# A graph-and-mixture kernel on one core: the prologue's degree pass shortened, its two roots computed in one chain, and layer 1's last block reordered

## The reference, cut to what matters

```python
xn = _layernorm(x, axis=-1)
x = x + _L0_gnn_ref(xn, edge_index, edge_weight, ...) + _L0_mix_ref(xn[None], ...)[0]
x = x + _L0_ffn_ref(_layernorm(x, axis=-1)[None], ...)[0]

def _gcn_conv(x, edge_index, edge_weight, W, b):      # used twice by _L0_gnn_ref
    ...                                               # self-loops of weight 1 are added
    deg = jax.ops.segment_sum(ew, col, num_segments=n)
    dis = jnp.where(deg > 0, jax.lax.rsqrt(jnp.where(deg > 0, deg, 1.0)), 0.0)
    norm = dis[row] * ew * dis[col]
    h = x @ W.T
    msg = h[row] * norm[:, None]
    return jax.ops.segment_sum(msg, col, num_segments=n) + b

def _block(x, edge_index, edge_weight, g, bln, W, b):
    h = _layer_norm(x, g, bln)
    return x + jax.nn.relu(_gcn_conv(h, edge_index, edge_weight, W, b))
```

## Time and profile before

| | us |
|---|---|
| median of 3 runs (lowest, highest) | 4452.32 (4449.44, 4452.76) |
| the profiled execution's own time | 4450.62 |
| its span, first to last instruction | 4448.9 |
| prologue, up to the first gather | 309 |
| layer 1, up to the first gather of layer 2 | 2038 |
| layer 2 | 2102 |

### The profile page before, as it was taken

How to read it: one execution, slowest core, us unless ns; L and a number is a source line. 1 busy time by engine, 2 the same in 40 slices (tenths; PEclk the granted TensorE clock), 3 DMA queues, 4 the chain that set the end, 5 groups by cost and what they waited for, 6 DMA issues and landing times.

```text
span 4448.9 us, 94972 instructions
## 1 busy us (share of the span) xinstructions
PE 3639.6 (82%) x27016; PEld 3069.7 (69%) x27017; DVE 2477.9 (56%) x8820; ACT 1205.1 (27%) x3172; POOL 3147.3 (71%) x3542
## 2 busy tenths in 40 slices
PE   4876776776776676777777999999999999999998
PEld 3765555655565565555555888888888887888877
DVE  7544544554554554545454665665566665666555
ACT  1330010100100110010013444444444444444434
POOL 4447777777777777777766777777777777777771
PEclk9988888888988888888888999999999999999999
DMA  4034444443444444444443343443344343344431
GB/s 143 29 105 120 130 129 120 129 130 115 129 130 120 128 131 125 125 129 127 119 119 106 116 117 110 118 118 111 114 118 118 110 118 115 114 118 115 117 107 42
DMA packets 256030, 515.37 MB, mean 116 GB/s; under 512 B 61465, under 2 KB 154017, under 8 KB 255969
## 3 DMA queue, kind: packets, MB, share of 16 engines
q0 software_dynamic: 151392, 413.60, 32.8%
q1 hardware_dynamic: 104576, 101.17, 7.0%
HBM read 474.81 MB, written 39.71 MB: 116 GB/s over the span
## 4 chain that ended last, share of the span: by engine, by line
PE 47%; DVE 17%; issue 10%; POOL 8%; DMA 7%; ACT 2%; DVEq 2%; SPq 0%; POOLq 0%; ACTq 0%
PE bank L1199 45%; POOL gs L549 8%; DMA gr<-h_d,idx_r 6%; DVE ss L966 4%; PE bank L1222 1%; DVE rstd L730 1%; DVE rstd L731 1%; DVE rstd L729 1%; DVE st L738 1%; DVEq L966 1%; DVE w L1097 1%; ACT bank L710 1%; DVE u L747 1%; ACT L710 1%; DMA out<-u 1%
## 5 line engine op out<-in xcount | busy, mean ns | idle before, releaser
L549 POOL DMA_INDIRECT gs<-h_d,idx_all x3038 | 2901.9, 955 | 951.3 <-issue 655.6
L1199 PE MATMUL bank<-gs,ss 128*128 128x256 f32 x6272 | 1585.7, 399 | 13.7 <-DMA gs<-h_d,idx_all 12.5
L1199 PEld LDWEIGHTS bank<-gs,ss 128*128 128x128 f32 x6272 | 1210.5, 201 | 191.2 <-DMA gs<-h_d,idx_all 21.5
L966 DVE TENSOR_SCALAR ss<-iw,dst_f,ew 128x128 f32<-128x128 f32 x3152 | 882.4, 358 | 115.8 <-PE bank L1199 67.9
L710 ACT ACTIVATE bank<-bank,eb1c 128x128 f32<-128x128 f32 x1632 | 455.6, 342 | 703.2 <-PE bank L1199 686.3
L1199 PE MATMUL bank<-experts,w 128*128 128x256 f16 x4896 | 616.8, 279 | 23.3 <-DVE w L1097 22.6
L1199 PE MATMUL bank<-w,experts 128*128 128x128 f16 x9792 | 613.8, 219 | 1.2 <-DVE w L1103 1.2
L1199 PEld LDWEIGHTS bank<-w,experts 128*128 128x128 f16 x9792 | 571.1, 98 | 48.7 <-issue 16.6
L1199 PEld LDWEIGHTS bank<-experts,w 128*128 128x128 f16 x4896 | 475.9, 100 | 101.0 <-DVE w L1097 32.6
L1199 PE MATMUL bank<-gr,sr 128*128 128x256 f32 x232 | 114.4, 587 | 449.6 <-DMA gr<-h_d,idx_r 449.4
L1097 DVE SCALAR_TENSOR_TENSOR w<-bank,w 128x512 f16<-128x512 f32 x408 | 280.7, 688 | 279.0 <-ACT w L713 274.5
(11 more groups left out here) (260 smaller groups left out, 3588.2 us busy)
## 6 DMA issues: line engine op xcount, KB each, us to landing
gs<-h_d,idx_all POOLq DMA_INDIRECT x3038
hself<-h_d SPq DMA_DIRECT2D x100, 128.0 KB, 3.3
ew_in<-in_eW SPq DMA_DIRECT2D x49, 168.0 KB, 2.4
out<-u SPq DMA_DIRECT2D x51, 128.0 KB
u<-xn_d SPq DMA_DIRECT2D x50, 128.0 KB
h_d<-u SPq DMA_DIRECT2D x50, 128.0 KB
u<-x_d SPq DMA_DIRECT2D x50, 128.0 KB
u<-r_d SPq DMA_DIRECT2D x50, 128.0 KB
```

What stands on the lines that cost most here:

```text
L549: pool.indirect_dma_start(gs[:, n, :], None, table[:, :], bass.IndirectOffsetOnAxis(ap=idx_all[:, w, n:n + 1], axis=0)).then_inc(s[f"main_ ...
L966: m = dve.tensor_scalar(ss[:, slot + j, :], iw[:, :], dst_f[:, bass.ds(c, 1)], ew[:, bass.ds(c, 1)], ALU.is_equal, ALU.mult)
L1199: return pe.matmul(out_ap, lhsT, rhs, start=first, stop=last, **kw)
```

## The change

It has these parts.

1. **Start of the prologue.** The statistics begin when the first three of the seven transfers of `x` have landed, and are written out instead of looped. Both inverse roots come from one chain of double width (`two`). The scaling of the weights, the copies of `hb`, `w1bias` and `u8` go from DVE to ACT, ahead of `xn_tile(0)`. POOL's addition of 128 to all source indices goes; each gather now has a constant offset (`element_offset`) instead.
2. **The loop over blocks.** POOL no longer copies the indices (DVE does, between L893 and L897) nor the quarter numbers: it subtracts a prepared pair `tile_qn` while it fetches the column. PE's bounds are read after `w6`'s product instead of ahead of it.
3. **End of the prologue.** The last fold stands ahead of block 48's products; DVE, not POOL, takes the last seven inverse roots; the last write of seven blocks is cut into four and three.
4. **Layer 1.** In all blocks the bias of the next row's product is put ahead of its turn (`next_h_bias`). In the last block the last messages and the rest come ahead of `w1`'s products, the next row's products ahead of `w2`'s, the next row is normalised alone, and its store stands ahead of the store of `r`. The waits ahead of `table2` stay.

```diff
             for i in range(0, W, XG):
...
+                             ).then_inc(s["x_first" if i < X_FIRST * XG else "x_in"], 16)
...
-            sp.wait_ge(s["h_dve"], W - H_DVE)
-            h1_rows(W // XG - 1)
+            for t, n in ((H_DVE, 4), (H_DVE + 4, XG - 4)):
+                sp.wait_ge(s["h_dve"], t + n - H_DVE)
+                sp.dma_start(h1_d[(t + 1) * P:(t + n + 1) * P, :].rearrange("(t p) d -> p t d", p=P),
+                             xh[:, t:t + n, :]).then_inc(s["h1_out"], 16)
...
+                if last:
+                    sp.wait_ge(s["h2_done"], W + 1)
+                    sp.dma_start(rows(h2_d, W), u4[:, :]).then_inc(s["h2_out"], 16)
                 sp.wait_ge(s["r_done"], w + 1)
...
-            pc.link(pool.tensor_scalar(src_row[:, :], src_row[:, :], P, None, ALU.add))
...
                 lo = own_column(pool, t)
-                pool.tensor_copy(idx_all[:, bass.ds(t, 1), :].rearrange("p a c -> p (a c)"),
-                                 src_row[:, bass.ds(lo, OWN)]).then_inc(s["idx_listed"], 1)
-                pool.tensor_copy(tile_q, iota_qb[:, bass.ds(t * Q, Q)]).then_inc(s["tile_q_set"], 1)
                 after, off = degree_columns(pool, t)
-                pool.wait_ge(s["tile_q_set"], t + 1)
                 with pool.Fori(after - 1, lo + (OWN - DEG + FRONT), 1) as c:
-                    pool.tensor_copy(own_qn, dst_qn[:, :, bass.ds(c, 1)].rearrange("p a c -> p (a c)")
-                                     ).then_inc(s["rest_own"], 1)
+                    pool.tensor_tensor(own_qn, dst_qn[:, :, bass.ds(c, 1)].rearrange("p a c -> p (a c)"),
+                                       tile_qn[:, bass.ds(t, 1), :].rearrange("p a c -> p (a c)"),
+                                       ALU.subtract).then_inc(s["rest_own"], 1)
...
-            root_seed(2)
-            for _ in range(NEWTON):
-                root_step(2)
-            root_end(2)
...
-                            bass.IndirectOffsetOnAxis(ap=idx_all[:, w, n:n + 1], axis=0)).then_inc(s[f"main_in{n}"], 16)
+                            bass.IndirectOffsetOnAxis(ap=idx_all[:, w, n:n + 1], axis=0),
+                            element_offset=P * D).then_inc(s[f"main_in{n}"], 16)
...
+            act.wait_ge(s["shift_ps"], 3)
+            act.copy(hb[:, 0, :], bank[1][0:1, 0:D])
+            act.copy(hb[:, 1, :], bank[2][0:1, 0:D])
+            act.copy(w1bias[:, :], bank[3][:, 0:HBLK])
+            for k in range(KB):
+                act.activation(w6[:, k, :], w6[:, k, :], ACT.Copy, scale=lncol[:, 0, k:k + 1])
+                act.activation(w7[:, k, :], w7[:, k, :], ACT.Copy, scale=lncol[:, 2, k:k + 1])
+                a = act.activation(w1[:, KB + k, :], w1[:, KB + k, :], ACT.Copy, scale=mixcol[:, 0, k:k + 1])
+            a.then_inc(s["weights_set"], 1)
+            act.wait_ge(s["shift_ps"], 4)
+            act.copy(u8[:, :], wide(2)).then_inc(s["weights_set"], 1)
             act.wait_ge(s["stats_set"], 1)
...
+            both, minus_half, root, tmp = (v[:, :] for v in two)
+            one, onto = slice(0, W), slice(W, 2 * W)
+            ch.link(dve.tensor_scalar(both[:, one], var_all[:, :], EPS, None, ALU.add))
+            ch.link(dve.scalar_tensor_tensor(out=both[:, onto], in0=both[:, one], scalar=EPS, in1=var_all[:, :],
+                                             op0=ALU.mult, op1=ALU.add))
+            inv_sqrt(dve, ch, both, minus_half, root, tmp)
...
+                dve.tensor_copy(idx_all[:, bass.ds(t, 1), :].rearrange("p a c -> p (a c)"),
+                                src_row[:, bass.ds(lo, OWN)]).then_inc(s["idx_listed"], 1)
                 dve.tensor_tensor(oh_node[b], iota_nc.unsqueeze(1).to_broadcast(shape), own_n.unsqueeze(2).to_broadcast(shape),
...
+            inv_sqrt(dve, ch, deg, mh, y, tmp)
+            dve.tensor_tensor(dis[:, 1 + CUTS[2]:], dis[:, 1 + CUTS[2]:], y, ALU.mult).then_inc(s["dis_set"], 1)
             keys(W - 1)
             rows_h(W - 1)
...
+                if last:
+                    z_ins, = layer_norm(dve, tc, (u5[:, :], u3[:, :]))
+                    z_ins.then_inc(s["z1_done"], 1)
+                    dve.wait_ge(s["y1_ps"], w + 1)
+                    y_ins, = layer_norm(dve, tc, (wide(4), t_c[1][:, :]))
...
+                    if last and k == 6:
+                        messages(w, v, PIECES - 1)
+                        rest_messages(*rest_table(pe, 0, w))
...
+                        if last:
+                            next_h_turn(W)
+                            next_h(W)
                         pe.wait_ge(s["hr_done"], HBLK * (w + 1))
```

More of the change, by code:

```diff
@@ L45 @@
 DCOL = NCOL + FRONT
-EDGE_LINKS = 7
+EDGE_LINKS = 6
 HEADS, HD = 8, 32
@@ L62 @@
 XG = 7
+X_FIRST = 3
 CUTS = (0, 4 * XG, 6 * XG, W)
@@ L1068, in window1 @@
                 dve.tensor_tensor(u6[:, :], t_c[1][:, :], t_c[0][:, :], ALU.add).then_inc(s["r_done"], 1)
-                assert tc.n == tc.per, tc.n
+                assert tc.n == tc.per + (LN_LINKS if last else 0), tc.n
             with dve.Fori(0, W - 1) as w:
```

125 lines of the change are left out of this document (65 added, 60 removed).

## The result

| | before | changed |
|---|---|---|
| median of 9 runs (lowest, highest) | 4452.32 (4449.44, 4453.63) | 4439.58 (4436.16, 4440.58) |
| profiled execution's own time, span | 4450.62, 4448.9 | 4436.16, 4434.5 |
| ratio of the times, 95% interval | | 0.9971 (0.9962 to 0.9981) |

A forecast was written before the change was run, and what follows sets the result against it. POOL's gathers were taken to bound layer 1, and a dependent chain the prologue. Terms −9.0 − 10 − 1 + 0 − .5 = −20.5 took 4450.62 to 4430.1, median 4431.8, stated as 4431; range 4420 to 4445.

The forecast's parts named there:

- the first two rivals: Whole kernel: the loop gives only 3, total 4438, chance .20; or the prologue's start gives only 3, 4437, chance .08.
- Start: Start of the prologue, up to PE's first `u,t_b`: 9.0 us gained, bounds 4 and 10.
- The loop: Prologue's loop over blocks: 10 us gained, POOL's part .33 shorter per block, DVE paying .19 for a copy.
- the early mode: Loop's first blocks, POOL ahead: 4.02 becomes 4.2 a block, +2.5 over 13 blocks; then 14 more at 4.2, −7.0.
- the late mode: Loop behind the first roots, POOL late: .1 a block, ten blocks −.9, second roots −1.2, last ones −.3.
- My own sign of being wrong: Any of: early blocks staying at 4.0 or over 4.4, gathers' mean moving over .01, first gather less than 12 earlier.
- the lock: Loop's blocks with POOL late: DVE and POOL exclude each other at a shared port pair, so 2.4 gained instead of 6.
- End of the prologue: From the last block's roots and scalings to the first gather: 1 us gained, bounds 0 and 2.5.
- Layer 1's body: Layer 1's gathers: 0 change, as POOL gets no added instruction; bounds −.02 and +.02 a gather, ∓31.
- Last block: Layer 1's last block: .5 gained, the store of `r` becoming last instead of the new row's; bounds −1.5 and +1.
- The slower rival: Layer 1: the constant offset lengthens each of 1,577 gathers, at .02 each +31.5, total 4462; chance .05.
- POOL stays ahead through the roots: Prologue: the loop gains 17 and the prologue's end 2.5, total 4422; chance .12.

The follow-up runs named there:

- a2: The changed kernel without the gathers' constant offset; POOL adds 128 to the source indices in its preparation as before. Median 4441.54, ratio .9969 of the kernel before.
- a4: The changed kernel with the copy of the source indices in the degree loop moved from DVE back to POOL. Median 4443.39, ratio .9971 of the kernel before.
- a8: The changed kernel with the first two groups' roots moved from POOL to DVE, in four pieces each. 6269.93 against the changed kernel's 6289.92; ratio .9881 of before.
- a1: The changed kernel with the next row's bias product put back behind the turn, ahead of w7's products. Median 4445.05, ratio .9979 of the kernel before.
- a5: The changed kernel with layer 1's last block in its old order, bias still moved; run twice. Medians 6284.76 and 6282.28, ratios .9900 and .9877 of before.

## Why the prediction was right, and where it was not

The direction and the range held, and by its parts the likeliest case; the size was 21 for a measured 12.7. The result, 4439.6, lies nearer to the 4438 and 4437 of the first two rivals than to 4431, but what they describe did not occur: the loop gave 9.4 and not 3, the start 9.7 and not 3. Two losses that no case had, 2.5 at the start and 4.0 in layer 1, took the number there.

- **Start: right, then in part given back.** 9.0 forecast at the first `u,t_b`, 9.7 measured. The parts differ: the statistics began 8.5 earlier, not 5.5, since POOL's addition had held DVE's work in front of them by 3.0 (a2), but they met the last loads for 1.17, and the roots ended at 56.7 instead of 54.2. I stopped counting at `u,t_b`. PE's clock rose 6.0 behind it instead of .9, since it rose only 4.6 earlier than before, and this took 2.5.
- **The loop: the sum about right, by luck.** 9.4 from block 3 on for 10, but its errors cancel: the early mode came out 2.3 better than forecast and the stretch behind it .6, the roots 1.1 worse and the late mode 2.3. The copy on DVE, 2.5 forecast for the blocks up to 15, left +.2 there; a4 puts it at .44 up to block 15 and 1.4 up to 28. My own sign of being wrong, an early mode that stays at 4.0, was all but met: 4.05 from block 3 to 15. The stretch from 15 to 28 gave 7.6 for 7, which I had counted as 14 blocks and which are 13. In the late mode I had .1 a block and the second and last roots, 2.4 in all; .1 was left. That the lock takes back what POOL saves there was the argument, and the rows fit it (POOL's first two short operations took .85 a block before and .98 now); no run takes the lock away, so it isn't shown that the lock alone does it. a8 shows that lateness, once there, stays: with the roots off POOL it doesn't fall behind up to block 42.
- **End of the prologue: right**, 1.1 for 1. The last scalings ended at 283.77 (forecast 282), 11.05 behind block 48's start instead of 14.80, so 3.7 earlier; only 1.1 of it reached the first gather, and the DMA engines were full in between, at 346 GB/s.
- **Layer 1's body: the step that failed.** "It adds no instruction to POOL", so 0, with 31 to either side for the constant offset. It is +4.0, and not the offset (a2): more gathers start where DVE's operations lengthen them, which is 4.1 by their sum. "What PE, DVE or ACT do there costs nothing so long as no gather waits longer" was the step: the gathers' waits stayed the same, and they themselves got longer. The bounds held it by luck, since they were for something else; and .02 each was twice the spread of .009 between the two forms that it names. a1 shows that such meetings can cost 13 more. Which place of the bias gives which meetings, and why, is open.
- **Last block: mechanism right, size not.** `r` did take over as the last store, 18.2 behind the last rest for 17.8 forecast. The .5 is .1 in the traces, and a5 makes the new order 1.0 worse than the old one with the moved bias. What the moved bias does for the old order, about 1.1, I had not counted.
- The slower rival, a dearer gather by the offset, is refuted. The rival "POOL stays ahead through the roots" was not reached by the change, but is what a8 does: 8.5.

So of the 20.5 forecast, 2.2 went to PE's clock and the smaller terms of the prologue (17.8 for 20.0), 4.0 to the gathers, .4 to the last block, and layer 2 gave .6: 14.4. The remaining 1.7 to the medians is that of the two profiled executions against their medians (3.4 below for the changed kernel, 1.7 before).

## What to carry to other kernels

Where one engine bounds a long stretch, "no instruction added" is not a price of nothing: look at which operations of the other engines meet its instructions, and count its long ones by what runs beside them. An engine that is just quick enough can be put behind by one side job and stay behind; moving the side job (8.5 us here) was worth more than shortening each round. When a gate waits for several transfers, the order of the queue that holds them counts as much as the waits: a wait moved behind the gate gave 1.2, the store with it 5.9, both at layer 2's first gather; neither is shown in the total.

## What the runs showed of the hardware that I had not expected

- A gather issued by POOL takes .95 us, and 1.00 to 1.28 where it starts during certain DVE operations, at mostly the same places in every block; layer 1 took 2017, 2021 or 2035 us by the gathers' length alone. None of 621, 709 and 639 gathers that started with DVE idle was over .97 us. During the selection matrices (.3 us, one wide operand) nearly only those were that started .10 to .20 us into one.
- On two chips the changed kernel took 42% longer. The gathers' packets ended as early as elsewhere (2.42 us behind the issue for 2.43), but signals between engines came late while POOL issued gathers: 7.14 us in the median from PE's last product to DVE's reading, for .14. The moved bias product alone was worth .96% there (.9904, .9872 to .9937), while the prologue's times were those of the other chips.
- The granted clock of PE rose only 4.6 us earlier when the first `u,t_b` came 9.7 earlier: `wk`'s four products took 2.06 in block 1 and 1.11 one block later, where before block 0's took 2.07 and block 1's 1.11.
